# Eight GpSimd operations for the selectors, the verdict on VectorE, an ungated first threshold and an earlier flag read in a top-k attention kernel

## The reference

```python
draft = jnp.einsum('bhqd,bhkd->bhqk', qr, kr)
draft = draft + jnp.where(causal_future, neg, jnp.asarray(0.0, dtype))
num_remain = max(min(Sq, MIN_REMAIN), Sq - int(Sq * MASK_OUT))
_, draft_indices = jax.lax.top_k(draft, num_remain)
mask = jnp.full((B, H, Sq, Sq), neg, dtype)
mask = mask.at[b_idx, h_idx, s_idx, draft_indices].set(0.0)
mask = jnp.where(causal_future[None, None, :, :], neg, mask)
scores = jnp.einsum('bhqd,bhkd->bhqk', qr, kr) / np.sqrt(HD) + mask
attn = jax.nn.softmax(scores, axis=-1)
```

## Time and profile before

| | us |
|---|---|
| median of 3 runs | 4233.72 (4233.6 to 4235.52) |
| span of the profiled execution | 4232.6 |
| phase A, to the first `go` | 610.4 |
| phase B, first to last `go` | 3236.0 |
| phase C, the rest | 386.2 |

### The profile page before, as it was taken

One profiled execution on the slowest core, in us unless ns is written; L12 is line 12 of the kernel. 1 busy time (PEld: TensorE's weight loads), 2 busy tenths in 40 slices (PEclk: granted clock), 3 DMA queues, 4 the chain that ended last, 5 costly groups with the idle time before them and its releaser, 6 DMA issues. The chain is left out here.

```text
span 4232.6 us, 55872 instructions
## 1 busy us (share of the span) xinstructions
PE 3367.7 (80%) x15864; PEld 1556.6 (37%) x15864; DVE 3153.8 (75%) x6185; ACT 2685.2 (63%) x4577; POOL 2008.4 (47%) x5916
## 2 busy tenths in 40 slices
PE   6999947787688677886877688888677888887998
PEld 3444423333233333332333233333333333333444
DVE  4667758888788688987876888888688888772333
ACT  1222137788588688886876688888688888872111
POOL 1222236555357665544576555546675554572000
PEclk9999968898899788998987899999878899998998
DMA  3112120000010110001001000010010000002211
GB/s 113 64 63 80 60 57 17 11 9 9 7 21 16 24 26 12 10 7 21 13 18 32 12 10 10 9 21 13 23 29 12 10 7 9 12 15 94 75 75 45
DMA packets 221756, 124.01 MB, mean 29 GB/s; under 512 B 188164, under 2 KB 206852, under 8 KB 221316
## 3 DMA queue, kind: packets, MB, share of 16 engines
q1 hardware_dynamic: 221316, 119.36, 10.0%
HBM read 76.28 MB, written 42.99 MB: 28 GB/s over the span
## 5 line engine op out<-in xcount | busy, mean ns | idle before, releaser
L901 PE MATMUL banks<-pT,v_sb 128*65 128x512 f32 x2176 | 1182.2, 627 | 30.9 <-ACT oT L1005 29.6
L990 ACT ACTIVATE pT<-banks 128x512 f32<-128x512 f32 x1088 | 634.2, 591 | 514.4 <-PE banks L873 509.2
L848 PE MATMUL banks<-k_sb,q_sb 128*128 128x512 bf16 (+3 forms) x1280 | 504.6, 394 | 380.1 <-DVE sc L1156 344.1
L1156 DVE TENSOR_SCALAR_CACHE_REDUCE sc<-banks 128x1024 f32<-128x1024 f32 (+7 forms) x768 | 674.9, 904 | 70.6 <-PE banks L853 39.2
L1183 DVE MAX8 near<-keys 128x8 f32<-128x256 f32 (+14 forms) x480 | 653.5, 1361 | 17.2 <-DVE keys L1181 0.6
L981 ACT ACTIVATE junk<-sc,tt 128x256 fp8e4<-128x256 f32 (+14 forms) x480 | 597.5, 1246 | 54.0 <-POOL tt L1048 53.9
L981 ACT ACTIVATE junk<-sc,t_all 128x256 fp8e4<-128x256 f32 (+14 forms) x480 | 599.3, 1249 | 33.9 <-DVE sc L1156 32.0
L981 ACT ACTIVATE junk<-sc,tiny 128x256 fp8e4<-128x256 f32 (+14 forms) x480 | 595.3, 1246 | 11.8 <-DVE sc L1168 11.8
L867 PE MATMUL banks<-q_sb,k_sb 128*128 128x512 bf16 x1088 | 444.1, 408 | 189.8 <-ACT pT L990 69.2
L850 PE MATMUL banks<-k_sb,q_sb 96*128 96x512 bf16 (+3 forms) x1280 | 494.1, 396 | 0.0
L873 PEld LDWEIGHTS banks<-eye,mk 128*128 128x128 bf16 x4352 | 358.6, 103 | 299.3 <-issue 68.9
(11 more groups left out here) (247 smaller groups left out, 4885.9 us busy)
## 6 DMA issues: line engine op xcount, KB each, us to landing
q_sb<-scratch_qk SPq DMA_DIRECT2D x896, 32.0 KB, 1.9
scratch_qk<-parts SPq DMA_DIRECT2D x16, 960.0 KB, 3.7
a_x<-in_x SPq DMA_DIRECT2D x16, 512.0 KB, 4.2
scratch_x<-a_x SPq DMA_DIRECT2D x16, 512.0 KB, 2.9
scratch_attn<-o_sb SPq DMA_DIRECT2D x128, 64.0 KB, 1.6
c_xn<-scratch_attn SPq DMA_DIRECT2D x16, 512.0 KB, 3.7
c_x<-scratch_x SPq DMA_DIRECT2D x16, 512.0 KB, 4.6
out<-c_x SPq DMA_DIRECT2D x16, 512.0 KB, 2.6
```

Source lines behind the costliest of these rows:

```text
L848: nc.tensor.matmul(r_slot(n)[:, j:j + wj], q_sb[:, p % QS, 0, h, :], k_sb[:, group[p] % 2, 0, col:col + wj], start=True, stop=False)
L901: nc.tensor.matmul(psum[0:VP, 6, :], v_sb[:, group[p] % 2, kb, :], pT[:, n % PTS, :], start=(kb == 0), stop=(kb == blocks[p] - 1)).then_in ...
L990: nc.scalar.activation(pT[:, tn % PTS, :], psum[:, 4 + n % 2, :], ACT.Exp, scale=SCALE)\
L1156: v.tensor_scalar(sc[:, p % SCS, h, c * CHUNK:c * CHUNK + w], r_slot(n)[:, 0:w], 0.0, None, ALU.add, ALU.max, accum_out=mx[:, p % 4, c, h: ...
```

## The change

Four edits, all in the search of phase B.

1. `selectors` has 8 operations for 13. The error is kept in half units (`steps` is now 2o+1), the selectors are a midpoint and a difference, and a relative margin GAP goes into the difference. `directions` compares with `is_ge`. `judge` is gone from GpSimd; after `dk`, VectorE waits for its own result, and forms the verdict in 2 operations, ahead of the differences. Rows whose count is right are judged by the same product now.
2. `first_update` steps always; the threshold comes after three operations instead of six, and two products for `second_update` are formed behind it. `second_update` has 12 operations for 13, six `link` waits for eight.
3. `fold` has four operations for six: the maximum isn't negated there; TensorE turns it with a negated identity.
4. `read_flag` stands ahead of the second mask, not the fourth; TensorE's `flags` waits in another order. `fall_back` has four operations fewer on its first part.

```diff
-                d0, q0, mv, gate = (dd[:, p % 3, j, :] for j in range(4))
+                d0, qst, mv, q0 = (dd[:, p % 3, j, :] for j in range(4))
...
-                    gp.tensor_tensor(q0, d0, d0, ALU.mult)
                     link(gp.tensor_tensor(mv, d0, st, ALU.mult))
-                    link(gp.tensor_scalar(gate, q0, (WINDOW - 0.4) ** 2, None, ALU.is_gt))
-                    link(gp.tensor_tensor(mv, mv, gate, ALU.mult))
                     gp.tensor_tensor(tt[:, p % 3, 0, :], t0, mv, ALU.add).then_inc(sm["t1"], 1)
+                    link(gp.tensor_tensor(q0, d0, d0, ALU.mult))
+                    gp.tensor_tensor(qst, q0, st, ALU.mult)
+                    link(gp.tensor_scalar(q0, q0, 1.0, None, ALU.max))
...
-                    gp.tensor_scalar(den, q0, 1.0, None, ALU.max)
-                    gp.tensor_tensor(mv, d1, st, ALU.mult)
+                    gp.tensor_tensor(mv, d1, qst, ALU.mult)
                     link(gp.tensor_tensor(nd, d0, d1, ALU.mult))
+                    gp.tensor_scalar(one, q1, (WINDOW - 0.4) ** 2, None, ALU.is_gt)
                     link(gp.tensor_scalar(nd, nd, 0.0, None, ALU.min))
-                    link(gp.tensor_tensor(den, den, nd, ALU.subtract))
+                    link(gp.tensor_tensor(den, q0, nd, ALU.subtract))
+                    gp.tensor_tensor(mv, mv, one, ALU.mult)
                     link(gp.tensor_tensor(den, den, b.minus[:, :], ALU.pow))
-                    gp.tensor_scalar(one, q1, (WINDOW - 0.4) ** 2, None, ALU.is_gt)
-                    link(gp.tensor_tensor(den, den, q0, ALU.mult))
-                    link(gp.tensor_tensor(mv, mv, one, ALU.mult))
                     link(gp.tensor_tensor(mv, mv, den, ALU.mult))
...
-                    link(gp.tensor_scalar(rest, mx[:, p % 4, 0, :], -1.0, None, ALU.mult))
-                    link(gp.tensor_copy(part[0], rest))
-                    link(gp.tensor_tensor(less, rest, part[0], ALU.subtract))
-                    link(gp.tensor_copy(part[1], less))
-                    link(gp.tensor_tensor(rest, less, part[1], ALU.subtract))
-                    gp.tensor_copy(part[2], rest).then_inc(sm["mf"], 1)
+                    most = mx[:, p % 4, 0, :]
+                    link(gp.tensor_copy(part[0], most))
+                    link(gp.tensor_tensor(less[:, :], most, part[0], ALU.subtract))
+                    link(gp.tensor_copy(part[1], less[:, :]))
+                    gp.tensor_tensor(part[2], less[:, :], part[1], ALU.subtract).then_inc(sm["mf"], 1)
...
+                    link(gp.tensor_scalar(d, sgn[:, p % 3, 2, :], b.tab[:, tile_of[p], TAB_TURN:TAB_TURN + 1], None,
+                                          ALU.subtract))
+                    link(gp.tensor_scalar(a, d, 1.0, -1.0, ALU.min, ALU.max))
+                    link(gp.tensor_tensor(a, a, d, ALU.mult))
                     link(gp.tensor_tensor(u, steps, wide(a), ALU.subtract))
+                    gp.tensor_tensor(q, u, u, ALU.mult)
+                    link(gp.tensor_scalar(w, u, GAP, None, ALU.subtract))
+                    link(gp.tensor_scalar(sel[:, p % 2, 0, :, :], q, 4.0, 0.5, ALU.is_lt, ALU.mult))
+                    gp.tensor_tensor(sel[:, p % 2, 1, :, :], sel[:, p % 2, 0, :, :], w, ALU.mult).then_inc(sm["sel"], 1)
...
-                    if searching(j):
-                        judge(j)
...
                     v.tensor_reduce(dk[:, p % 2, :, :], pick[:, :, :, :], AX.X, ALU.add).then_inc(sm["dk"], 1)
+                    dve.wait_ge(sm["dk"], chosen[p + 1])
+                    link(v.scalar_tensor_tensor(verdict[:, :], dk[:, p % 2, 1, :], 1.0, dk[:, p % 2, 0, :], ALU.min, ALU.mult))
+                    v.tensor_scalar(bad[:, p % 2, :], verdict[:, :], 0.0, None, ALU.is_le).then_inc(sm["bad"], 1)
...
-                        if searching(j) and h + 1 == REP:
+                        if searching(j) and h == 1:
                             read_flag(j)
```

More of the change, by code:

```diff
@@ L46 @@
 (TAB_Z, TAB_SLOPE, TAB_K, TAB_COUNT, TAB_OPEN, TAB_INVN, TAB_TURN, TABS) = range(8)
+GAP = 2.0 ** -19
 U = 3
@@ L84, in shape_constants @@
     future = np.triu(np.full((P, P), MASKED, np.float32), 1)
-    steps = np.tile(np.arange(8) + 0.5, (P, REP)).astype(np.float32)
+    steps = np.tile(2 * np.arange(8) + 1, (P, REP)).astype(np.float32)
     return {"rope": rope, "tab": tab, "eye": eye, "future": future, "steps": steps}
@@ L731, in phase_b @@
         mx = sb("mx", [P, 4, 2, REP])
-        nm = sb("nm", [P, 2, REP])
+        less = sb("less", [P, REP])
         sgn = sb("sgn", [P, 3, 3, REP])
@@ L744, in phase_b @@
         dk = sb("dk", [P, 2, 2, REP])
-        gp4 = sb("gp4", [P, 4, REP])
+        verdict = sb("verdict", [P, REP])
         bad = sb("bad", [P, 2, REP], BF16)
@@ L752, in phase_b @@
         fbi = sb("fbi", [P, 8], I32)
[L753 removed]
+        one_js = sb("one_js", [P, 2])
         n16 = sb("n16", [P, 16])
@@ L1077, in fold @@
                         pool.wait_ge(sm["mf"], p)
-                    rest, less = nm[:, 0, :], nm[:, 1, :]
                     part = [mm[:, p % 2, :, ONES_AT + n] for n in range(PARTS_OF_MAX)]
@@ L1089, in selectors @@
+                    link(gp.tensor_copy(part[0], most))
+                    link(gp.tensor_tensor(less[:, :], most, part[0], ALU.subtract))
+                    link(gp.tensor_copy(part[1], less[:, :]))
+                    gp.tensor_tensor(part[2], less[:, :], part[1], ALU.subtract).then_inc(sm["mf"], 1)
                 def selectors(p):
                     pool.wait_ge(sm["sign"], sign_no[p, 2, REP - 1] + 1)
-                    d, sg, a, ga, far = (js[:, p % 2, j, :] for j in range(5))
-                    u, q, m = (ev[:, j, :, :] for j in range(3))
+                    if p >= 2 and chosen[p - 1]:
+                        pool.wait_ge(sm["dk"], chosen[p - 1])
@@ L1093, in selectors @@
+                    d, a = (js[:, p % 2, j, :] for j in range(2))
+                    u, q, w = (ev[:, j, :, :] for j in range(3))
                     steps = b.steps[:, :].rearrange("p (h o) -> p h o", h=REP)
-                    link(gp.tensor_scalar(d, sgn[:, p % 3, 2, :], 0.5, b.tab[:, tile_of[p], TAB_COUNT:TAB_COUNT + 1],
-                                          ALU.mult, ALU.add))
-                    link(gp.tensor_scalar(sg, d, 1.0, -1.0, ALU.min, ALU.max))
-                    link(gp.tensor_tensor(a, d, sg, ALU.mult))
@@ L1141, in _ @@
                 link(v.tensor_copy(wide_steps[:, 0:8], b.steps[:, 0:8]))
-                link(v.tensor_scalar(wide_steps[:, 8:16], b.steps[:, 0:8], 8.0, None, ALU.add))
+                link(v.tensor_scalar(wide_steps[:, 8:16], b.steps[:, 0:8], 16.0, None, ALU.add))
                 link(v.memset(v_sb[:, :, :, HD:VP], 1.0))
@@ L1217, in fall_back @@
                         then(v.tensor_reduce(c, heads_bad[:, :], AX.X, ALU.max))
-                        then(v.tensor_scalar(which, c, 0.5, None, ALU.subtract))
+                        then(v.tensor_scalar(which, c, 0.5, 0.5, ALU.mult, ALU.subtract))
                         hb = dve.value_load(fbi[0:1, 7:8], min_val=0, max_val=REP - 1)
@@ L1221, in fall_back @@
                         s = sc[:, p % SCS, head, 0:w].rearrange("p o w -> p (o w)")
-                        sign1, dist, some, far = (one_js[:, j:j + 1] for j in (1, 2, 3, 4))
+                        dist = one_js[:, 1:2]
                         u, m, low, mid = (eq[:, j, :] for j in range(4))
```

47 lines of the change are left out of this document (12 added, 35 removed).

## The result

| | before | after |
|---|---|---|
| median, four runs of each on one chip | 4234.19 us | 4166.69 us (4165.99 to 4168.26) |
| ratio, 95% interval | | 0.984 (0.9827 to 0.9853) |
| span of the profiled execution | 4232.6 us | 4165.5 us |
| phase A, B, C | 610.5, 3235.9, 386.2 | 608.2, 3173.0, 384.3 |

The change takes 67.5 us off, 62.9 of them in phase B. The forecast was 38 us off (4196).

A forecast was written before the change was run, and what follows sets the result against it. No engine was taken to bound all of phase B: GpSimd held narrow steps; VectorE, ScalarE or TensorE others. Per pair 8.8 + 4 - 1.2 - 2.9 = 8.7, four times 35, plus 3 for the fallback: 38 us off, 4196; range 4138 to 4252.

The forecast's parts named there:

- GpSimd in the narrow steps: Tiles 1 to 4: shorter GpSimd work brings the second threshold and differences sooner, 8.8 us for a pair of groups.
- the flag read: Before `go`: early read gains 0.3 to 0.7 us a step up to tile 9, 0.2 above; descending 13 loses 1.9.
- the descending tiles 15 to 9: Wide descending steps: 1.7 us lost at tile 13, less at 11, 12, 14, 15; 2.9 lost for a pair.
- ascending 11 to 15: Wide ascending steps: verdict costs 0.45 us each against waits for signs, half counted; 1.2 us lost for a pair.
- First threshold in the middle steps: Ascending tiles 7 to 10: the threshold comes 0.7 us sooner, and the verdict lies in that wait.
- the fallback: Four of 120 steps take it, each losing four operations of some 0.2 us: 3 us gained in all.
- The verdict: Two VectorE operations ahead of the differences: 0.45 us a step, covered where the differences wait for the threshold anyway.
- A: Rival: VectorE is the bound wherever it waits now, so all its waits count; 92 us off, 4142; chance 0.2.
- B: Rival: VectorE stalls at the early flag read, 38 us in mostly wide steps; slower, 4266; chance 0.17.
- C: Rival: another engine takes over, ScalarE in the narrow steps, where half of 35 us is gained; 4221; chance 0.11.
- D: Rival: the number of steps taking the fallback moves, 15 to 18 us for each step more; chance 0.05.
- E: Rival: GpSimd holds VectorE up now; without judge the differences run quicker, 55 us on top, 4141; chance 0.02.

The follow-up runs named there:

- flag late: Changed kernel with the flag read put back ahead of the fourth mask: 4181.3 us, ratio 0.9872.
- GpSimd long: Changed kernel with eighteen idle operations put into GpSimd's lists, to make them as long as before: 4214.4 us, ratio 0.9956.
- skip long: Changed kernel with four idle memsets, each with its drain, put into the fallback that most steps skip: 4197.8 us, ratio 0.991.
- verdict on GpSimd: Changed kernel with the verdict moved from VectorE to GpSimd behind the second update, as three operations: 4158.5 us, ratio 0.9822.

## Why the prediction was right, and where it was short

The direction and the largest term (GpSimd in the narrow steps) were right. The size was short by 30 us, and two things make up most of that: the flag read brings 15 us net where the sum had at most 4, and the skipped code, worth some 13, stood in no sum and no rival. That the time fell into the range owes nothing to an account of these two, so it is in part luck. The sum also has a slip: its 2.9 us for the descending tiles 15 to 9 is 3.2 by its own terms, which makes 37 us of 38.

Phase B by kind of step, in us, from `go` to `go` summed over the four pairs of groups. A gain is positive; the last four columns say what a step gets longer by when one part of the change is taken back.

| steps | forecast | gained | flag late | GpSimd long | skip long | verdict on GpSimd |
|---|---|---|---|---|---|---|
| narrow, 1 to 4 | 35 | 43.2 | 16.4 | 42.9 | 11.9 | -6.6 |
| ascending 5 to 10 | 16 | 31.9 | 11.9 | 6.7 | 14.8 | -1.0 |
| ascending 11 to 15 | -5 | -9.6 | -1.4 | -3.5 | 5.9 | 0.5 |
| descending 15 to 9 | -12 | -2.8 | -5.7 | 1.7 | 6.0 | -0.8 |
| descending 8 to 5 | 0 | -0.5 | -1.5 | -1.1 | -4.3 | -1.2 |
| phase B with tile 0 | 38 | 62.9 | 16.7 | 43.8 | 31.3 | -10.1 |

*GpSimd in the narrow steps: right.* The place and the size hold: 42.9 us by the run, 35 by the sum; the limit that follows is the normalisation in the step shown. The parts overlap here, and the columns add to more than was gained, since each lengthens the same steps. Descending tile 2 gained 4.4 us a step for 2.2; two of its four steps ended in such a pause.

*First threshold in the middle steps: too large.* The term had 0.7 us in 16 steps, 11 us; GpSimd's whole shortening is worth 6.7 there. Part of it is the duration: three operations for six were to save 1.0 us, but they take 1.73 us in the mean of all steps for 1.62. At best they take 0.83 us. But 183 of the 360 now run beside a mask of VectorE, as in the rows shown above, and 172 of these take over 0.35 us; of the other 177, 11 do. The threshold is still earlier because GpSimd starts on it earlier; ScalarE's wait for it is 4.1 us for 53.9.

*The skipped code: missing.* The forecast costed the fallback by its four executions, 3 us, of which 1.2 were found. That 116 steps jump over it, and how far, was not in the sum. Without the steps that run it, its weight is some 11 us for nine instructions fewer in the kernel before, and 25 for eight more in the changed one. Of the 31.9 us that the ascending tiles 5 to 10 gained, 16.6 were such pauses. The rows of `go` had them, with up to 3.3 us under "issue", and the forecast passed over them. The Trainium skill (Advanced Engine Details and Errata, section "ISA Cache") gives two lines of 16 KB, 256 instructions each. The trace's packets are 8192 bytes, and a skip of 143 instructions already pauses, so the step seen here is half of that line.

*The flag read: direction right, both terms too small.* The loss was placed at descending 13 and sized 1.7 us; the run gives 1.5 there. But descending 8 and ascending 14 lose as much, where the sum had nothing through the flag: 28 us of loss in all, at most 13 in the sum. The gain elsewhere is 45 us, 12 in the sum, which had about half a microsecond of covered branch in the ascending tiles 5 to 10 and none in the narrow ones.

*The verdict: the duration right, the path wrong.* It takes 0.42 us (`dk` ends at 2965.71, the differences start at 2966.02, and without it they would overlap `dk` by 0.1). By the sum it costs in the wide steps and is covered in the narrow. The two runs say otherwise: taken off VectorE it gives nothing in the wide and 6.6 us in the narrow, 3.3 of them moved pauses, and put behind the differences 9.3 in the narrow, 0.5 of them pauses. At two of the three narrow widths VectorE no longer waits for the threshold once GpSimd is shorter. A cover that the same change removes is no cover.

Adding up by medians: 47.7 for GpSimd, 14.6 for the flag, less 8 for the verdict, are 54 of the 67.5 us. The 13 left are about what the shorter skip is worth by itself in the kernel before, 14.0. The agreement is better than the interval of each term (5 us) and the overlap of the parts allow one to claim. Why ascending 11 to 15 lose 9.6 us instead of 5 stays open: no single part taken back gives it back. The late flag returns 1.4 (6.1 at tile 14, less what 13 and 15 lose), the long GpSimd 3.5 and the verdict behind the differences 4.5; they were not run together.

*The rivals.* A's mechanism (a wait of VectorE is worth its length) held for the narrow steps alone: there the threshold wait fell by 47.7 us and the shorter GpSimd is worth 42.9, elsewhere it fell by 30 and is worth 4. On the flag A was nearer than the forecast, with 48 us of open time behind the read for the 45 found. B's stalls did what it described, with 28 us for its 38, and lost against the gain. C: ScalarE did not take over; its signs cost VectorE the same 200 us. D: the same four steps take the fallback. E, that GpSimd holds VectorE up, fell by VectorE's differences of one width in the kernel before, the changed one, and the one with GpSimd long again:

```profile
L1168 DVE TENSOR_SCALAR sc<-sc,tt 128x1280 f32<-128x1280 f32 x32 | 26.2, 883 | 12.9 <-POOL tt L1069 12.9
```

```profile
L1148 DVE TENSOR_SCALAR sc<-sc,tt 128x1280 f32<-128x1280 f32 x32 | 26.2, 882 | 4.0 <-POOL tt L1068 4.0
```

```profile
L1173 DVE TENSOR_SCALAR sc<-sc,tt 128x1280 f32<-128x1280 f32 x32 | 26.2, 881 | 7.9 <-POOL tt L1073 7.9
```

They take 883, 882 and 881 ns, with GpSimd busy 2008, 1282 and 2076 us: VectorE is not held up. GpSimd is. In the kernel before, its two-input operations of 128x4 take 0.20 us where VectorE does nothing, and 0.73 in the median of the 275 that run wholly beside a difference; the rows beside the masks above show the same. The Trainium skill (SBUF — State Buffer, "Who interferes with whom") says that VectorE in a 2-port mode and GpSimd lock each other out, whichever starts first holding the other up whole. The trace agrees for GpSimd as the one held up, and shows no difference of VectorE that is.

*What was to be seen.* The threshold wait was to be under 30 us, and is 29.8. TensorE was not to wait for the verdict, and doesn't. The wait at the flag read was to be 40 to 80 us, and is 88.2; ahead of `go` under 30, and is 22.3. Descending tile 13 was to be longer by 1 to 2 us, and is by 1.2; tiles 4 and 3 shorter by 1.4 to 2.4, and are by 2.1 and 1.9. Descending tile 8 was to be unchanged, and is 1.2 longer: the early read.

## What to carry to other kernels

Code that a branch skips is part of the step: count the instructions it jumps over, and look at every pause of an engine that no semaphore ended for an instruction packet inside it. An early read of a flag is worth it only where the flag is early too, so its place can differ from step to step; here that gave 12 us more, and 24 together with a skip shorter than one packet. Cost a new operation on the path as the change leaves it, not as the old waits show it. And when an engine's work moves to another time, look at what it will run beside: half as many operations on GpSimd took as long beside VectorE's masks as all of them had elsewhere.

## Of the hardware, not expected

A jump by VectorE over 143 instructions paused in 15 to 19 of 116 steps, over 135 in 6, over 134 (in the kernel before) in 11, over 126 in one. Each pause that is counted holds one 8192-byte instruction packet that begins 1.7 to 2.1 us ahead of the next operation. The pause can be covered: where masks are queued behind the flag read, the engine works them off while the jump is under way (3.8 us from flag to `go`, 1.51 left open behind 2.29 us of masks).

GpSimd pays where it runs beside VectorE's differences, `keys` and masks: a 128x4 operation took 0.91 to 0.98 us beside masks of 1.09 us and 0.19 after them, while the masks kept their length (3.28 us for three, 3.27 before). Beside VectorE's `MAX8` and its reads from the accumulators the same operations kept their 0.20 us.
